# Still-weight products on TensorE ahead of waits, and the middle groups of a transformer block written out

## The reference, cut to what matters

```python
h = patches(x) @ W.T + b                                    # 64 x 92 x 128
h = h + attention(layernorm(h))     # 8 heads; softmax, mixed over heads, normalised over heads, times v
h = h + ffn(layernorm(h))
# ffn
scores = softmax(xf @ gate_w.T); topk_w, topk_i = top_k(scores, 2); topk_w /= topk_w.sum(-1)
combine = zeros(T, 8).at[rows, topk_i].add(topk_w)          # routing weights
eo = relu(xf @ w1[e] + b1[e]) @ w2[e] + b2[e]               # each of 8 experts, for each token
y = sum_e combine[:, e] * eo[e] + relu(xf @ sw1 + sb1) @ sw2 + sb2
```

## Time and profile before

| | us |
|---|---|
| median of 3 runs (718.61 to 721.12) | 719.9 |
| the profiled execution | 721.9 |
| its span, first to last instruction | 719.8 |
| PE busy | 636.0 (88%) |
| VectorE busy | 503.5 (70%) |
| ScalarE busy | 447.5 (62%) |
| GpSimd busy | 419.6 (58%) |
| mean granted TensorE clock | 0.945 |

### The profile page before, as it was taken

How to read it: one execution, slowest core, us unless ns; L and a number is a source line. 1 busy time by engine, 2 the same in 40 slices (tenths; PEclk the granted TensorE clock), 3 DMA queues, 4 the chain that set the end, 5 groups by cost and what they waited for, 6 DMA issues and landing times.

```text
span 719.8 us, 17637 instructions
## 1 busy us (share of the span) xinstructions
PE 636.0 (88%) x5704; PEld 584.8 (81%) x5704; DVE 503.5 (70%) x1431; ACT 447.5 (62%) x1430; POOL 419.6 (58%) x568
## 2 busy tenths in 40 slices
PE   4888699898989899898989999898989989896666
PEld 3787598888979799888979888897979988885565
DVE  3744868678776867677686877777686767766532
ACT  3376576676757667575658667575767667575312
POOL 2555448475664748376574848476474937566513
PEclk9789899999999999999999999999999999999976
DMA  6000020202021020202002020202103020202020
GB/s 205 22 2 23 7 97 7 97 21 95 21 83 33 1 94 21 95 21 92 25 17 99 0 95 21 95 21 84 32 1 97 18 95 2 96 2 81 16 90 15
DMA packets 16697, 36.67 MB, mean 51 GB/s; under 512 B 1504, under 2 KB 13728, under 8 KB 14624
## 3 DMA queue, kind: packets, MB, share of 16 engines
q1 hardware_dynamic: 16672, 36.35, 15.4%
HBM read 33.14 MB, written 3.20 MB: 50 GB/s over the span
## 4 chain that ended last, share of the span: by engine, by line
PE 70%; DVE 20%; issue 4%; ACT 3%; DMA 2%; POOL 1%; SPq 0%; ACTq 0%; POOLq 0%; DVEq 0%
PE ps_mix L616 15%; PE ps_fill L409 12%; PE ps_fill L410 10%; PE ps_fill L411 10%; PE ps_dots L605 9%; PE ps_av L624 6%; PE ps_fill L560 5%; DVE key L999 4%; DVE shift_l L988 2%; DVE aT L1043 2%; DVE x2T_lo L1100 1%; PE ps_fill L717 1%; DVE hot L994 1%; ACT x2T_hi L838 1%; DMA spread<-weights 1%
## 5 line engine op out<-in xcount | busy, mean ns | idle before, releaser
L481 POOL TENSOR_TENSOR act_split_lo<-act,act_split_hi 128x736 fp32r<-128x736 f32 (+1 forms) x80 | 127.6, 1603 | 16.8 <-ACT act_split_hi L821 16.8
L1172 POOL TENSOR_TENSOR sum<-sq 92x384 f32<-92x384 f32 x64 | 64.6, 1009 | 114.5 <-ACT sq L763 114.5
L755 ACT ACTIVATE ex<-ps_dots,negmax 128x92 f32<-128x92 f32 x384 | 124.3, 342 | 4.8 <-DVE negmax L1024 4.4
L616 PE MATMUL ps_mix<-mixk,probs 128*92 128x128 f32 x768 | 110.4, 300 | 13.0 <-DVE aT L1045 13.0
L616 PEld LDWEIGHTS ps_mix<-mixk,probs 128*92 128x92 f32 x768 | 97.2, 177 | 19.1 <-issue 12.8
L1166 POOL TENSOR_TENSOR probs<-ex,rinv 128x552 f32<-128x552 f32 x64 | 71.0, 1110 | 49.5 <-DVE rinv L1030 49.4
L1119 DVE SCALAR_TENSOR_TENSOR act<-ps_fill,b_neg,spread 128x368 f32<-128x368 f32 x128 | 70.7, 590 | 24.7 <-PE ps_fill L411 17.8
L755 ACT ACTIVATION_READ_ACCUMULATOR ex<-ps_dots,negmax 128x1 f32 x384 | 81.3, 212 | 0.0
L605 PE MATMUL ps_dots<-xT,yT 128*64 128x92 f32 x1536 | 74.5, 247 | 5.0 <-ACT ex L755 2.6
L605 PEld LDWEIGHTS ps_dots<-xT,yT 128*64 128x64 f32 x1536 | 65.0, 138 | 9.2 <-ACT ex L755 3.8
L1043 DVE TENSOR_TENSOR aT<-ps_mix,arstd 92x360 f32<-92x360 f32 x128 | 61.7, 522 | 6.8 <-ACT arstd L773 4.5
(11 more groups left out here) (173 smaller groups left out, 1737.1 us busy)
## 6 DMA issues: line engine op xcount, KB each, us to landing
spread<-weights SPq DMA_DIRECT2D x16, 1472.0 KB, 6.2
xin<-in_x SPq DMA_DIRECT2D x16, 320.0 KB
out<-ostage SPq DMA_DIRECT2D x16, 128.0 KB, 1.9
act<-w_raw SPq DMA_DIRECT2D x2, 576.0 KB, 7.7
out<-ostage SPq DMA_DIRECT2D x16, 56.0 KB, 1.6
xin<-in_x SPq DMA_DIRECT2D x16, 52.0 KB
qkv<-qk_raw SPq DMA_DIRECT2D x1, 512.0 KB, 5.1
spread<-tok_raw SPq DMA_DIRECT2D x1, 256.0 KB, 3.6
```

Source lines behind the costliest of these rows:

```text
L481: eng.tensor_tensor(lo, act1[:, two, :], hi.bitcast(F32), ALU.subtract).then_inc(units_ready, 1)
L616: last = pe.matmul(ps_mix[0:N, c // HALF, o:o + 128], probs[:, (s - 1) % 2, c, :], mixk[:, :, :].rearrange("p g i -> p (g i)"), start=True ...
L755: last = act.activation(ex[:, s % 2, c, :], ps_dots[:, c // HALF, o:o + N], ACT.Exp, bias=negmax[:, c:c + 1], accum_out=sums[:, s % 2, c:c ...
L1172: pool.tensor_tensor(sum4[:, :, :, :], sq[:, :, 0:4, :], sq[:, :, 4:8, :], ALU.add)\
```

## The change

Four things are changed. `keep_busy` issues a number of matmuls on PE ahead of a step, into `ps_dots`, from a tile that doesn't change any more: at the start zeros that VectorE clears first (`act1_split`), at the end the expert weights (`w1_split`). KEEP_BUSY says ahead of which steps and how many. Ahead of CT, in groups 1 to 15, eight such products of the expert weights with themselves (128 x 368) go into CT's own bank, and the wait for `route` now comes behind them. Nothing reads these products. And the loop is gone: groups 2 to 13 are written out like the others, so that group numbers and semaphore values are known when the program is built.

```diff
+KEEP_BUSY = {(FIRST, "XE"): 13, (FIRST, "TK"): 10, (FIRST, "TX"): 13, (LAST - 2, ("mix", 0)): 8, (LAST - 2, "TH2"): 4,
+             (LAST - 2, "TX2"): 15, (LAST - 2, "RT"): 6, (LAST - 1, "Z0"): 25}
+ROUTE_BUSY = 8
...
-            for G in range(FIRST + 1, STEADY):
-                iteration(G)
-            with eng.Fori(STEADY, END) as G:
+            for G in range(FIRST + 1, END):
                 iteration(G)
...
+            def keep_busy(step, G):
+
+                count = KEEP_BUSY.get((G, step), 0) if isinstance(G, int) else 0
+                if count:
+                    if G == FIRST:
+                        pe.wait_ge(still_tile, 1)
+                        tile = act1_split[0]
+                    else:
+                        pe.wait_ge(exp_ready, B)
+                        tile = w1_split[0]
+                    columns = tile[:, 0:4, :].rearrange("p e w -> p (e w)")
+                    for _ in range(count):
+                        pe.matmul(ps_dots[:, 0, 0:W], columns[:, 0:128], columns[:, 0:W], start=True, stop=True)
...
+                keep_busy(step, FIRST)          # in prepare, and at the head of do
...
-                if step == "CT":
-                    pe.wait_ge(route, N_ROUTE * (g + 1))
...
                 elif step == "CT":
+                    columns = w1_split[0][:, 0:4, :].rearrange("p e w -> p (e w)")
+                    for _ in range(ROUTE_BUSY if g >= 0 and G < LAST - 2 else 0):
+                        pe.matmul(ps[:, 0:W], columns[:, 0:128], columns[:, 0:W], start=True, stop=True)
+                    pe.wait_ge(route, N_ROUTE * (g + 1))
                     transposes(step, G, [(ps[:, R * t:R * t + R], combine[:, t, :], ident) for t in range(TILES)])
...
+            dve.memset(act1_split[0][:, 0:1, :].bitcast(F32), 0.0).then_inc(still_tile, 1)
```

More of the change, by code:

```diff
@@ L365, in audio_tower @@
         prep = sem("prep")
+        still_tile = sem("still_tile")
         dots_ready = sem("dots_ready")
@@ L631, in do @@
             def do(step, G):
+                keep_busy(step, G)
                 if isinstance(step, tuple):
```

## The result

The changed kernel takes 693.0 us in the median (692.41 to 693.29, four runs); the kernel before, run beside it on the same chip, takes 719.25 (718.61 to 721.12, four runs). The ratio is 0.963, with an interval of 0.9609 to 0.9651: 3.7% faster. The forecast was 692.3. The profiled execution after took 693.01 us with a span of 691.2, against 721.9 and 719.8 before.

What follows compares the result with a forecast made beforehand. PE with its own dependencies sets the period, and low-clock stretches are paid in full. Terms 17.6 + 0.5 + 1.9 + 2.2 + 2.4 + 3.0 = 27.6 us off 721.9 give 694.3, less 2.0 for the median 692.3; 8 in 10: 685 to 703.

Steps and rivals of the forecast that it cites:

- B: Group 1's CT: eight products leave 2.9 us of its 4.3 us wait idle; gain 0.5 us, between nothing and 1.6.
- D: The start: products of zeros in the waits before XE, TK and TX raise the clock; gain 2.2 us, from -1 to 4.6.
- A: Eight products before CT, groups 1 to 15: fit the wait, cost nothing, remove 11 clock drops of 1.6 us; gain 17.6 us.
- R1: Rival, behind CT: the clock falls all the same, the eight products gain 0; 710 us, at worst 719; chance 0.10.
- C: Groups 2 to 13 written out: 12 "issue" waits before the first dots go, 0.16 us each; gain 1.9 us, 1.4 to 2.4.
- R4: Rival, the loop: each turn hides a DMA fetch of 1.36 us, 14.4 us more gain; 678 us; chance 0.02.
- R2: Rival, start and end: the products there give nothing; 699.9 us; chance 0.19.
- E: The end, last group's routing: products in waits keep the clock up, combine 1.0 us earlier, CT too; gain 2.4 us, 0 to 2.6.
- F: The end, last experts: 25 products fill the 4.51 us wait before Z0, GpSimd is late next; gain 3.0 us, 0 to 3.5.
- R3: Rival, written-out groups: instruction fetching stalls PE, up to 6.2 us a group, 74 in all; 766 us; chance 0.04.

## Why the prediction was right

**How close the number is, and how much of that is luck.** The forecast was 692.3, the median 693.0. Two errors partly cancel. The terms came out 1.3 us too small: 27.6 forecast against 28.9 between the two profiled executions, most of it in B and D. And I took 2.0 us off because the profiled execution before was slower than its runs; the one after was not (693.01 against 693.0), so this term was 2.0 us of nothing. As runs of the kernel after spread over 4 us, an agreement to 0.7 is better than the sum deserves. What is right is the mechanism and the size of each part.

**What bounds the kernel.** PE with its own dependencies, and so a drop paid nearly in full (3.4 us at half speed is 1.7 us of work, and the period is 1.62 longer): the kernels with and without the drop differ in the period and hardly in anything else. VectorE is busy 370.5 us over twelve periods in both, ScalarE 329.8, GpSimd 306.7 to 306.9. But the dependencies lead over VectorE's routing chain, before and after, and one of its operations stands out there: `key` (L999 before, L1021 after), 128x24, takes 2.07 us on the chain where its like take 0.19. It starts beside an operation of GpSimd and ends within 0.05 us of GpSimd's next one (277.06 to 279.12 after, 286.50 to 288.57 before); no run tests whether that is the cause. And a drop is not paid everywhere: in a second profiled execution of the kernel after the clock also fell for 3.4 us at 628, behind a wait of 1.34 us before an RT, and the two stretches from CT of group 14 to the last CT took 70.3 us together, as in the first one, which has the same wait and no drop there.

**A, the eight products: 17.6 us.** Right in kind and size. Eleven of these thirteen stretches hold a turn of the loop, 1.9 to 2.3 us; taken from the 19.7 gained, that leaves 17.4 to 17.8. One drop is 1.62 us where I read 1.6 from the two kinds of period, and eleven are 17.8. The count of drops varies, eleven of thirteen in the kernel before and ten in the written-out one, so A is 16 to 18 us by execution. The eight do fit the wait, as sixteen do not. R1, that the clock falls all the same, was the open risk, because 0.64 us idle and three small transposes remain; it did not happen in any of the twelve middle periods, in eight profiled executions with eight products or more, and three products instead of eight leave 0.83 us more of idle time and still hold the clock. Why two or three periods of thirteen keep it with no products at all, behind the same wait, is not settled. It is no matter of chance period by period: in each of the three written-out kernels that have the drops, the three periods without one are neighbours. In the looped kernel the two lie six periods apart.

**B, group 1: 0.5 us.** The mechanism was partly missed. I let the eight products start when PE is idle; they had to wait 2.22 us for ScalarE to empty CT's bank, then ran at the low clock (2.82 us) and ended behind `combine`. Still the period came out 1.2 us shorter. The low stretch is as long as before, but 3.5 us of it lie behind the CT instead of 4.9; half of that difference, 0.7 us, and a turn of the loop, 0.2, are 0.9 of the 1.2 by this estimate. Before the CT, 13 products in a free bank do cure the stretch: the two kernels with them have group 1's period at 39.1 us. Together with D (below) the two give 3.85 us here, but 4.2 and 0.7 in the two other profiled executions of the same program, so the term has no fixed size.

**C, the loop: 1.9 us.** Measured 2.5 with the products (0.21 a turn) and 2.0 to 2.2 without (0.17 to 0.18). The row of "issue" waits, 2.4 us, was all there is of it. R4, by which each turn pays a hidden DMA trip, falls: the loop put back cost 2.5 us and not 16. The Trainium skill's sentence on taken branches ("Runtime: NRT & Kernel Launch", Instruction fetch mechanics) speaks of a target outside the fetched pages; no stall of that kind shows here in either form.

**D, the start: 2.2 us.** In the profiled execution 2.64, by the steps that I named: XE 0.12 later, TK's first product at 8.23 instead of 8.50, TX at 15.89 instead of 17.87. The products of zeros do raise the clock, which R2 doubted: the first TK product behind them takes 0.44 us in the row, where it took 0.67, and the twelve start 0.17 us apart instead of 0.31. What I did not see is that the start has no fixed length. The kernels with the fills at the start and at most eight products in group 1 reach the first CT at 83.5, 83.7, 84.2, 84.3, 84.5, 84.6 and 86.9 us, those without at 85.9, 86.1 and 87.0: 1.8 us apart in the mean, but the first seven up to 3.4 apart among themselves. The kernel with sixteen, at 89.8, is left out, because 2.45 us more of late products stand before its CT. So the 2.64 of one pair of executions agrees with my 2.2 by luck as much as by the sum. The start is also most of the spread of the kernel's times: with its gaps filled in the last version the spread falls from 4.2 us to 0.4.

**E, the end, routing: 2.4 us.** Measured 2.29. `combine` comes 32.3 us behind the CT before it, against 33.3 before: 0.9 us earlier, where I had 1.0. YF is over by then, CT follows `combine` after 0.15 us (667.27 to 667.42).

**F, the end, last experts: 3.0 us.** Measured 2.78. GpSimd's four operations run without a gap for 6.95 us, where the last waited 1.29 before, and GpSimd, not PE, is late next, as worked out: YF ends at 687.53 - 0.85 = 686.68, 1.34 us behind GpSimd's last (678.39 + 6.95 = 685.34); I had 1.15.

**The rivals.** R2, that the ends give nothing, is refuted by the two kernels with one half each: 700.5 without the end fills, which is near the 699.9 that I worked out for R2, and about 693 with them. R3, instruction fetching: packets on queue q8 go from 14 to 47 (I had guessed 14 and three per group, 50), 0.77 MB, and no period from group 2 to 13 is longer than 39.5 us. I had called q8 the one instruction queue; the page lists a second, q14, which goes from 11 to 34 packets, 0.28 MB. Nothing is seen to wait for either.

## What to carry to other kernels

Where TensorE sets the period and its mean clock is below 1, cut the trace into periods and compare two of different length: if the other engines' busy time is equal and only the clock differs, the difference is the price of a drop, and short waits around a few small operations are where to look, not only long ones. Fill them with products on data that is there, into a bank that is free at that moment, no more of them than the wait holds; a fill that waits for its bank can come too late, as in group 1. And where a kernel's runs spread more than its middle periods do, look at the clock in the start of a slow run: filling those gaps as well took 4 us of spread away here.

## What the runs showed of the hardware that I had not expected

- Waits of 1.39 and 0.64 us around three small transposes can be enough for the clock to drop for 3.4 us; they did so in ten or eleven periods of thirteen. Eight products of 8 columns left as many drops as none (nine in twelve periods), with 0.55 us of idle time before CT; three of 368 columns left 0.83 us idle and no drop. PE's idle time in the profile did not tell the two apart.
- Products whose operands are all zero raise the clock: behind thirteen of them, which began at 1.28 us, the eight transposes of XE take 0.83 us instead of 1.47.
- A turn of the hardware loop costs TensorE 0.17 to 0.21 us.
- The same program reached its first CT at 83.5, 84.5 and 86.9 us, with different gaps of its start punished. The Trainium skill ("TensorE: Matmul & The Clock Gate", What's actually happening) says that one kernel shows different numbers of slow products from run to run, by the phase of the clock gate when it starts; the three traces agree with the first half of that, at up to 3.4 us, and none shows the phase itself.
